# A gated cross-attention block: the softmax exponentials read PSUM head by head

## The reference

```python
x = x + tanh(g_xattn[0]) * xattn(layernorm(x), ctx)
x = x + tanh(g_ffn[0]) * ffn(layernorm(x))

# xattn: B=2, N=1024 rows, M=77 context rows, 8 heads of 64
attn = softmax(einsum('bhnd,bhmd->bhnm', q, k) * 64 ** -0.5, axis=-1)
out = einsum('bhnm,bhmd->bhnd', attn, v).reshape(B, N, 512) @ Wo + bo

# ffn: 256 -> 1024 -> 256, values rounded to 8 bits before each product
h = relu(fixed_quant(fixed_quant(x) @ w1q.T + b1q))
out = h_quantised @ w2q.T + b2q
```

## Time and profile before

| | us |
|---|---|
| median of 3 runs | 119.74 (119.52 to 121.28) |
| profiled execution, whole | 120.01 |
| its span in the profile | 118.2 |
| TensorE busy | 111.8 (95%) |
| VectorE busy | 97.7 (83%) |
| GpSimd busy | 89.1 (75%) |
| ScalarE busy | 76.4 (65%) |

### The profile page before, as it was taken

How to read it: one execution, slowest core, us unless ns; L and a number is a source line. 1 busy time by engine, 2 the same in 40 slices (tenths; PEclk the granted TensorE clock), 3 DMA queues, 4 the chain that set the end, 5 groups by cost and what they waited for, 6 DMA issues and landing times.

```text
span 118.2 us, 2898 instructions
## 1 busy us (share of the span) xinstructions
PE 111.8 (95%) x1012; PEld 102.1 (86%) x1012; DVE 97.7 (83%) x223; ACT 76.4 (65%) x169; POOL 89.1 (75%) x161
## 2 busy tenths in 40 slices
PE   7979997899999999999999999999999999999990
PEld 2659976899798999988999999999999999897870
DVE  3029798999999999989999999999797979648981
ACT  4137766869688894998667575748483819448420
POOL 4003587698796989898989978996899999988720
PEclk9999999999999999999999999999999999999999
DMA  4989799300000000000010002000200020020204
GB/s 80 315 247 386 280 375 399 152 0 8 0 3 0 6 3 0 0 6 0 0 74 15 6 0 89 0 3 6 89 0 0 3 89 6 0 89 8 88 13 165
DMA packets 5328, 8.87 MB, mean 75 GB/s; under 512 B 1191, under 2 KB 2242, under 8 KB 5186
## 3 DMA queue, kind: packets, MB, share of 16 engines
q1 hardware_dynamic: 5082, 8.34, 20.1%
q10 hardware_dynamic: 232, 0.34, 0.9%
HBM read 6.59 MB, written 2.10 MB: 73 GB/s over the span
## 4 chain that ended last, share of the span: by engine, by line
PE 52%; POOL 21%; DVE 14%; DMA 5%; issue 3%; ACT 1%; SPq 1%; POOLq 0%; DVEq 0%; ACTq 0%
PE sc_ps L841 15%; PE of_ps L878 12%; PE h_ps L910 7%; DMA wq_sb<-in_L_xattn_Wq_dram 5%; POOL hid L362 5%; POOL x_sb L383 4%; PE of_ps L925 4%; POOL probs L300 4%; POOL rstd L310 3%; POOL yq L316 3%; DVE probs L614 3%; PE tr_ps L853 3%; DVE mx L609 3%; DVE den L621 2%; DVE pT L650 1%
## 5 line engine op out<-in xcount | busy, mean ns | idle before, releaser
L841 PE MATMUL sc_ps<-a_sb,xT 128*128 128x308 f32 x192 | 31.1, 311 | 0.7 <-DVE probs L614 0.7
L878 PE MATMUL of_ps<-u_sb,pT 128*128 128x256 f32 x240 | 30.9, 281 | 0.1
L878 PEld LDWEIGHTS of_ps<-u_sb,pT 128*128 128x128 f32 x240 | 29.5, 188 | 0.3 <-issue 0.3
L841 PEld LDWEIGHTS sc_ps<-a_sb,xT 128*128 128x128 f32 x192 | 27.4, 188 | 1.4 <-issue 1.2
L438 ACT ACTIVATE probs<-probs,rstd 128x616 f32<-128x616 f32 x16 | 13.1, 818 | 23.0 <-DVE probs L614 23.0
L481 ACT ACTIVATE hid_q<-h_ps,b1z 128x256 int8<-128x256 f32 x58 | 24.5, 494 | 3.6 <-PE h_ps L910 3.6
L300 POOL TENSOR_TENSOR probs<-probs,rden 128x616 f32<-128x616 f32 x16 | 19.5, 1221 | 1.9 <-DVE rden L624 1.9
L362 POOL CAST hid<-hid_q 128x512 bf16<-128x512 int8 x27 | 15.8, 611 | 2.0 <-ACT hid_q L481 2.0
L910 PE MATMUL h_ps<-x2T,w1T 128*128 128x256 bf16 x128 | 16.7, 274 | 0.0
L609 DVE TENSOR_REDUCE mx<-sc_ps 128x8 f32<-128x616 f32 x16 | 12.6, 787 | 2.8 <-PE sc_ps L841 2.7
L614 DVE TENSOR_TENSOR probs<-sc_ps,mx 128x616 f32<-128x616 f32 x16 | 12.8, 800 | 0.5
(11 more groups left out here) (124 smaller groups left out, 175.8 us busy)
## 6 DMA issues: line engine op xcount, KB each, us to landing
w_sb<-in_L_ffn_w_dram SPq DMA_DIRECT2D x2, 1024.0 KB, 10.9
out_dram<-x_sb SPq DMA_DIRECT2D x7, 256.0 KB, 2.5
x_sb<-in_x_dram SPq DMA_DIRECT2D x4, 256.0 KB, 8.0
x_sb<-in_x_dram SPq DMA_DIRECT2D x1, 1024.0 KB, 9.8
wq_sb<-in_L_xattn_Wq_dram SPq DMA_DIRECT2D x1, 512.0 KB, 5.8
wv_sb<-in_L_xattn_Wv_dram SPq DMA_DIRECT2D x1, 512.0 KB, 7.8
wo_sb<-in_L_xattn_Wo_dram SPq DMA_DIRECT2D x1, 512.0 KB, 8.6
wk_sb<-in_L_xattn_Wk_dram SPq DMA_DIRECT2D x1, 256.0 KB, 3.4
```

The lines of the kernel that those rows point to most:

```text
L841: ins = nc.tensor.matmul(sc_ps[:, a, 0:HALF], xT[:, T % 2, p, c, :], a_sb[:, q, T // TB, c, HALF * a:HALF * a + HALF], start=first, stop=last)
L878: ins = nc.tensor.matmul(attn_ps, pT[:, T % 2, p, P * c:P * c + P], u_sb[:, q, MC * (T // TB) + c, :], start=first, stop=last)
```

## The change

For tiles 2 to 15 but 5 (`HEAD_EXP`), ScalarE reads the scores in PSUM itself, one head an instruction, as exp(rstd x s + bias), with bias = -rstd x max. VectorE no longer subtracts for these tiles; it makes the eight biases of a row with one small instruction, `minus_max`. Tiles 0, 1 and 5 keep the old way. The bank of scores is released by the last of the eight exponentials (`exp_done`). VectorE's `center` for these tiles stands ahead of the first statistics of tile s+5 in place of behind them.

```diff
+HEAD_EXP = tuple(T for T in range(2, TILES) if T != 5)
...
+        minus_max = sb("minus_max", [P, 2, H])
...
+        def centered_by(T):
+            return len([t for t in range(T + 1) if t not in HEAD_EXP])
...
             def exponentials(T):
                 act.wait_ge(rstd1_ready, T + 1)
-                act.wait_ge(centered, T + 1)
-                nc.scalar.activation(probs_v(T), probs_v(T), ACT.Exp, scale=rstd1[:, T:T + 1]).then_inc(exp_done, 1)
+                if T in HEAD_EXP:
+                    act.wait_ge(minus_max_ready, T + 1 - centered_by(T))
+                    act.wait_ge(pT_psum, T - 1)
+                    for h in range(H):
+                        ins = nc.scalar.activation(probs_v(T)[:, h, :], sc_v[:, h // 4, h % 4, :], ACT.Exp,
+                                                   bias=minus_max[:, T % 2, h:h + 1], scale=rstd1[:, T:T + 1])
+                    ins.then_inc(exp_done, 1)
+                else:
+                    act.wait_ge(centered, centered_by(T))
+                    nc.scalar.activation(probs_v(T), probs_v(T), ACT.Exp, scale=rstd1[:, T:T + 1]).then_inc(exp_done, 1)
...
                 dve.wait_ge(max_ready, T + 1)
+                if T in HEAD_EXP:
+                    dve.wait_ge(rstd1_ready, T + 1)
+                    nc.vector.tensor_scalar(minus_max[:, i, :], mx[:, i, :], rstd1[:, T:T + 1], -1.0, ALU.mult,
+                                            ALU.mult).then_inc(minus_max_ready, 1)
+                    return
...
                 if live(s - 6):
                     result(s - 6)
+                if s + 2 in HEAD_EXP:
+                    center(s + 2)
                 if 1 <= s and live(s + 5):
                     stats_first(s + 5, s + 6)
-                if live(s + 2):
+                if live(s + 2) and s + 2 not in HEAD_EXP:
                     center(s + 2)
...
             def scores(T):
                 pe.wait_ge(xT_high, T + 1)
-                if T >= 1:
-                    pe.wait_ge(centered, T)
+                if T - 1 in HEAD_EXP:
+                    pe.wait_ge(exp_done, T)
+                elif T >= 1:
+                    pe.wait_ge(centered, centered_by(T - 1))
...
                 else:
-                    pe.wait_ge(centered, TILES)
+                    pe.wait_ge(exp_done, TILES)
```

More of the change, by code:

```diff
@@ L225, in flamingo_kernel @@
         scores_ready, max_ready, centered, exp_done = sem("scores_ready"), sem("max_ready"), sem("centered"), sem("exp_done")
+        minus_max_ready = sem("minus_max_ready")
         den_ready, rden_ready, probs_ready = sem("den_ready"), sem("rden_ready"), sem("probs_ready")
```

## The result

The changed kernel takes 133.32 us (median of 4 runs, 131.36 to 134.53) against 119.63 (119.43 to 121.28): a ratio of 1.106, 95% interval 1.099 to 1.113. Every median here is of all runs and every ratio of the fast ones alone (runs within 1.5% of the fastest of their kernel; here 131.36 and 133.18), so the ratio puts the slowdown at 12.7 us where the medians have 13.7. The forecast was 126.4 us with a range to 130.5. The direction was right, the forecast slowdown about half of the measured one: 6.7 us against 13.7. The profiled execution is the shortest of the four, 131.36 us with a span of 129.5.

The account below looks back on a forecast made before the run. TensorE was taken to bound the steady steps at 5.82 us; waits for the exponentials, then a 5.91 us ring, pull the end by 6.65: 120.01 + 6.65 = 126.66, less 0.27 for the median, 126.4 us, range 122.8 to 130.5.

Parts of the forecast that it names:

- A head's cost: ScalarE's exponential over 77 columns from PSUM with two pointers: 458 ns, starts 326 ns apart, eight in 2.74 us.
- E: Length of one tile's block of eight exponentials on ScalarE, taken as 2.74 us.
- The early milestones: TensorE's score starts for tiles 3 to 8, forecast late by 2.14, 1.98, 3.45, 3.45, 3.71 and 5.30 us.
- The scaling: VectorE's instruction over eight columns that makes the biases: 0.16 us, replacing a 0.80 us subtraction, 0.64 us gained a tile.
- The ring: Steady steps: scores 1.94, to exponentials 1.13, exponentials 2.74, back to TensorE 0.10, together 5.91 us against TensorE's own 5.82.
- may hold tile 6 back by another 0.2, left out: VectorE's own order might delay tile 6 by another 0.2 us; not counted in the sum.
- sign of error: The prediction would be wrong if, among other signs, the steady step is above 6.1 us.
- rival 4: TensorE's clock falls after waits of some 2 us; a step adds up to 5.8 us, one fall giving 132; chance 0.04.
- Rival 3: ScalarE becomes the bound throughout: block of exponentials 3.27 us, ring 6.44 us, time 133.3 us; chance 0.13.
- rival 1: ScalarE fetches the second pointer beside the first: block 1.87 us, ring 4.98, time 121.3 us, within 2%; chance 0.09.

Follow-up runs that it names:

- the last experiment: Changed kernel with the maximum in PSUM, VectorE's result behind the maximum, and ScalarE's copy x2T ahead of both halves of the hidden rounding: 125.39 us, ratio 1.042.
- after: The changed kernel itself, with eight exponentials a tile, against the kernel before: 133.32 us, ratio 1.106.
- either edit alone: Changed kernel with VectorE's result behind the maximum and scaling (132.40 us), or with ScalarE's copy x2T ahead of both halves of the hidden rounding (132.54 us).
- both: Changed kernel with VectorE's result behind the maximum and scaling and ScalarE's copy x2T ahead of both halves of the hidden rounding: 131.27 us, ratio 1.094.

## Why the prediction was wrong, point by point

**A head's cost: right, a little high.** I had 458 ns, 326 apart, block 2.74; measured 437, some 305 apart, 2.56. The second pointer, 110 in my sum, is 84. The rule that I cited from the Trainium skill ("ScalarE: Activation LUTs", section "What ACT_TABLE_LOAD costs") gives the head exactly (436) and misses the overlap: by it the block is 2.84, the trace has 2.56. The shorter block makes the kernel faster than forecast. By my own price of E (1.2 us a tenth down to 2.65, 0.5 below) 0.18 us less is 1.5 us, 124.9; the last experiment, with nothing else against it, took 125.39.

**The early milestones: right in kind.** TensorE waits for the exponentials ahead of tiles 3, 5 and 7 by 1.96, 1.51 and 0.61 us, ahead of tile 8 by 1.14 (behind the copies of the second weight), and ahead of the tail's transpose by 1.17. The starts themselves were off where the table above says so, by the scaling (tiles 4 and 8) and the clock (tile 5), which are the next points. That these early stretches, and not the steady steps, carry most of the loss held too: 8.5 against 3.3 us.

**The scaling, "0.16 (0.05 either way)": failed.** It lasts 0.23 to 1.51 us. My row for it, the one-column scaling of the earlier trace rows, could not show this: it took its 0.14 us in the middle of a GpSimd addition (L383, 106.83 to 107.56), so the form of one column was not held where the one of eight is. The removed subtraction read PSUM and took 0.80 us all 16 times; its replacement reads SBUF. Cost: 2.3 us. I had bounded this term by the length of the instruction alone, and a small instruction sits in the ring with its whole wait.

**The ring, "5.91 us": failed, in kind.** I closed it through PSUM (scores, maximum, exponentials, scores) and left VectorE's own order out ("may hold tile 6 back by another 0.2, left out"). The ring that binds goes from the exponentials to the sum and through six more instructions of VectorE to the next biases: 6.13, and 6.34 where the scaling is stretched. A second, over two steps through ScalarE's copy `x2T`, is as long (12.46). Mine, with the measured block, is 1.94 + 1.13 + 2.56 + 0.10 = 5.73, below TensorE's 5.83. The hold of PSUM is a link of neither ring that binds: the hold alone leaves the step at 5.83, and the eight heads without it make the step 6.97. I named as a sign of error a steady step above 6.1; it is 6.2. Cost: 2.2 us.

**The clock, rival 4 at 0.04: a term put at nothing.** I forecast waits of some 2 us ahead of tiles 3 and 5, still took a clock of 1.00, and gave the other case a chance of 0.04. It fell in all four runs, in three of them by an amount that fits two falls. A fall costs about 1.4 us, not up to 5.8, since it ends within about 3.4 us: the stretch with it is 1.44 longer with the hold alone, 1.44 in after; the two falls of after are 2.7 together. What decides whether a wait of that length brings a fall is open, since the last experiment had one of 1.99 us and none. The rule in the prediction that idle stretches bring the lower level (the Trainium skill, "TensorE: Matmul & The Clock Gate", "Part 1: The HAM clock gate") was the better guide than the even 1.00 of the trace before, which had no such idle stretch.

**The sum.** 125.4, measured with everything removed, plus 2.2 for the rings, 2.3 for the scaling and 2.7 for the clock is 132.6 of the 133.3 measured. The profiled executions give a sum of their own. From the scores of tile 0 to the tail's transpose it is 98.26 us in after, 91.93 in the last experiment, and 92.84 in the forecast: 6.33 us for one fall (1.44), the scaling and the rings (4.89 together), less 0.91 where even the kernel without them beats the forecast (the shorter block, for the most part, is my estimate), less the 0.76 of the early start, is the 4.66 of the table. Rival 3 gave 133.3 as well, by a block of 3.27 and a ring of 6.44: that the number agrees is luck, the mechanism is refuted by the 2.56 in the trace. One slip in the working moves nothing: rival 1's ring is 5.04 by its own terms, not 4.98, below TensorE's step either way.

## What to carry to other kernels

When a change makes one link longer, follow it around through every engine's own order and not only through the buffer that it holds: list each ring through the new instruction, over one step and over two, and compare all with the bound step. When it replaces an instruction that reads PSUM by one that works in SBUF alone, look at what GpSimd runs at that moment, however small the new one is. And where a forecast has TensorE wait near 2 us, the sum needs a price for the clock: here 1.4 us a fall.

## What the runs showed of the hardware

- A VectorE scaling over eight fp32 columns, all in SBUF, ran 0.23 us or until a GpSimd instruction over 256 columns or more ended, up to 1.51 us (1.83 and 1.85 in other kernels), through two casts and an addition in a row. GpSimd's two-column product (0.70 us) did not hold it, and a scaling over one column was not held at all in the one place that shows it. With its input in PSUM it took 0.23 in 26 of 26.
- TensorE's clock fell to its lower level after single waits of 1.5 to 2 us, stayed there for about 3 us, and cost 1.4 us a fall; in some executions and not in others of the same kernel.
- One execution of a kernel ran TensorE's groups of scores in 6.01 us where 1.94 is usual, from the start and at a reported clock of 1.00: 388.13 us in place of 130.5.
- Eight exponentials over 77 columns each start some 305 ns apart and take 2.56 us from PSUM; from SBUF, with a bias of zeros, 2.85.
- Two rings of nearly equal length hide each other: six steady steps took 37.06 and 37.21 us with either edit alone and 35.08 with both, against 37.18.
